# Context passed in a second, turned order and loaded straight to the convolution's operand, in place of transposes on TensorE

## The reference

```
vr, x1r, x2r = v, ctx, ctx reshaped to (B=16, H=32, heads=8, L=512)
kv = vr[:, :, :, None, :] * x2r[:, :, None, :, :]      # 8 x 8 products per (b, h)
y  = causal convolution of kv with k[h] along L        # by FFT in the reference
y  = y + kv * skip[h, i]
out = einsum('bhijl,bhil->bhjl', y, x1r)               # context again
```

## Time and profile before

| what | value |
|---|---|
| median of 3 runs | 1280.31 us (1278.77 to 1292.66) |
| the profiled execution | 1288.01 us, span 1286.1 us |
| mean granted TensorE clock in it | 0.966 |
| TensorE busy | 1158.3 us, 90% of the span |
| VectorE, GpSimd, ScalarE busy | 837.4, 696.6, 547.5 us |
| HBM read, written | 152.65 MB, 43.83 MB |

### The profile page before, as it was taken

One profiled execution on the slowest core, in us unless ns is written; L12 is line 12 of the kernel. 1 busy time (PEld: TensorE's weight loads), 2 busy tenths in 40 slices (PEclk: granted clock), 3 DMA queues, 4 the chain that ended last, 5 costly groups with the idle time before them and its releaser, 6 DMA issues.

```text
span 1286.1 us, 18058 instructions
## 1 busy us (share of the span) xinstructions
PE 1158.3 (90%) x5369; PEld 887.2 (69%) x5369; DVE 837.4 (65%) x1369; ACT 547.5 (43%) x1012; POOL 696.6 (54%) x404
## 2 busy tenths in 40 slices
PE   3999999999999999999689999999888987998893
PEld 2777777777777777777578899996555654665561
DVE  1687787777777777787569994544554544555452
ACT  5455555556555655553411222223433433443341
POOL 4988898889889887995030000012443534445342
PEclk9999999999999999999989999999988989998997
DMA  6313322332233223321366343455999999999994
GB/s 194 86 52 102 102 77 76 102 102 78 75 102 101 80 74 102 102 62 50 107 158 193 98 117 104 122 152 160 277 277 291 290 272 283 289 302 284 283 277 55
DMA packets 88795, 196.51 MB, mean 153 GB/s; under 512 B 14983, under 2 KB 23943, under 8 KB 88624
## 3 DMA queue, kind: packets, MB, share of 16 engines
q1 hardware_dynamic: 73648, 159.84, 43.3%
q0 software_dynamic: 15104, 36.16, 12.3%
HBM read 152.65 MB, written 43.83 MB: 153 GB/s over the span
## 4 chain that ended last, share of the span: by engine, by line
PE 55%; DMA 24%; issue 8%; DVE 7%; ACT 2%; POOL 2%; SPq 1%; POOLq 0%; DVEq 0%; ACTq 0%
DMA out_dram<-o,idx_b 9%; PE Y L541 9%; PE Y L410 8%; DMA out_dram<-w,idx_b 8%; PE Y L412 8%; PE Y L411 8%; PE Y L414 3%; DMA stage<-xn_rows,idx_i 3%; DMA xn<-xn_rows 2%; DVE s L1146 2%; PE DX L393 2%; PE OT L559 2%; PE Y L630 2%; PE DX L559 2%; PE DX L433 2%
## 5 line engine op out<-in xcount | busy, mean ns | idle before, releaser
L969 POOL TENSOR_TENSOR ring<-vT,cT 128x1024 f32<-128x1024 f32 x128 | 249.1, 1957 | 77.9 <-ACT vT L738 49.5
L410 PE MATMUL Y<-split,toep 128*128 128x512 f32 x576 | 250.2, 434 | 9.7 <-POOL split L977 9.7
L1101 DVE TENSOR_TENSOR z<-Y,cT 128x1024 f32<-128x1024 f32 x128 | 156.1, 1220 | 126.8 <-PE Y L414 91.4
L977 POOL TENSOR_TENSOR split<-ring,split 128x1024 fp32r<-128x1024 f32 x96 | 229.8, 2394 | 0.4 <-ACT split L748 0.4
L412 PE MATMUL Y<-split,toep 128*128 128x512 f32 x576 | 228.7, 397 | 0.0
L411 PE MATMUL Y<-split,toep 128*128 128x512 f32 x576 | 228.4, 396 | 0.0
L630 PE MATMUL Y<-ring,xT 128*128 128x384 f32 x512 | 201.5, 520 | 9.1 <-DMA ring<-in_L_ffn_down_proj_dram 7.9
L1013 POOL DMA_INDIRECT stage<-xn_rows,idx_i x64 | 69.1, 1079 | 235.1 <-issue 219.1
L1106 DVE TENSOR_REDUCE o<-z 128x128 f32<-128x1024 f32 x128 | 154.4, 1207 | 1.1
L541 PE MATMUL Y<-split 128*128 128x384 f32 x768 | 152.9, 348 | 1.6 <-DVE split L1160 1.6
L410 PEld LDWEIGHTS Y<-split,toep 128*128 128x128 f32 x576 | 109.2, 190 | 39.4 <-issue 19.1
(11 more groups left out here) (152 smaller groups left out, 1913.1 us busy)
## 6 DMA issues: line engine op xcount, KB each, us to landing
ring<-_L_ffn_gate_up_proj_dram SPq DMA_DIRECT2D x64, 768.0 KB, 7.6
ring<-in_L_ffn_down_proj_dram SPq DMA_DIRECT2D x64, 384.0 KB, 10.2
gr<-filters SPq DMA_DIRECT2D x32, 512.0 KB, 3.8
stage<-in_x_dram SPq DMA_DIRECT2D x32, 256.0 KB, 3.5
stage<-in_ctx_dram SPq DMA_DIRECT2D x32, 256.0 KB, 3.8
x_rows<-stage SPq DMA_DIRECT2D x32, 256.0 KB, 2.9
xn_rows<-xn SPq DMA_DIRECT2D x32, 256.0 KB, 3.0
xn<-xn_rows SPq DMA_DIRECT2D x32, 256.0 KB, 3.8
```

The costliest lines, as they stand in the source:

```text
L410: pe.matmul(y, high, kv[:, s, 0, a, n], start=(a == 0), stop=False)
L969: pool.tensor_tensor(to.rearrange("p (b j i) -> p b j i", i=NH, j=NH), a, d, ALU.mult).then_inc(kvp_ready, 1)
L977: pool.tensor_tensor(kv[:, s, 1, c, :], kvp[c], kv[:, s, 0, c, :].bitcast(F32), ALU.subtract).then_inc(kv_ready, 1)
L1101: dve.tensor_tensor(zz[c % 2].rearrange("p (b j i) -> p b j i", j=NH, i=NH), YY[c % 2][:, :].rearrange("p (b j i) -> p b j i", j=NH, i=NH) ...
```

## The change

The host passes one more input, `turned(ctx)`: for each tile h a block of 128 x 512, whose row p holds, for chunk c and row n of the tile, the context at position c*128 + p. `load_turned(h, s)` copies that block to `cT[:, s]` by one transfer of the sync queue. The eight instructions a tile that made `cT` before are gone from TensorE (four loads of weights and four matmuls, L388), and ScalarE's eviction (L742). GpSimd waits for the transfer in place of the eviction. The wait for `z_done` moves from ScalarE to the sync queue. The loads of tiles 0 and 1 are issued in the set-up, ahead of the wait for `filters_out`; that of tile h+1 stands first in `iteration(h)`, before `load_filter(h + 1)`. The unturned context is loaded as before.

```diff
--- before.py
+++ after.py
@@ -54,7 +54,7 @@
 
 
 def build(nc, x, skip, ctx_in, k, gate_w, gate_up, down, sh_gate, sh_up, sh_down,
-          c_sq, c_order, c_slot, out):
+          c_sq, c_order, c_slot, ctx_turned, out):
     xn_rows = nc.dram_tensor("xn_rows", [T + CAP, LP], F32, kind="Internal").ap()
     x1_rows = nc.dram_tensor("x1_rows", [T, L], F32, kind="Internal").ap()
     chosen_rows = nc.dram_tensor("chosen_rows", [E, CAP], F32, kind="Internal").ap()
@@ -151,6 +151,7 @@
         dve_setup, k_turned, k_high, k_low, filters_out, pads_out = sem("dve_setup"), sem("k_turned"), sem("k_high"), sem("k_low"), sem("filters_out"), sem("pads_out")
         dve_turn, pool_turn = sem("dve_turn"), sem("pool_turn")
         w_ps, w_sb = sem("w_ps"), sem("w_sb")
+        cT_in = [sem("cT_in0"), sem("cT_in1")]
         tile_in, filter_in, g_ready = [sem("tile_in0"), sem("tile_in1")], sem("filter_in"), sem("g_ready")
         skip_in = [sem("skip_in0"), sem("skip_in1")]
         ln1_mean, ln1_var, ln1_sd, ln1_rstd = sem("ln1_mean"), sem("ln1_var"), sem("ln1_sd"), sem("ln1_rstd")
@@ -158,7 +159,7 @@
         skip_ready = sem("skip_ready")
         b_xT_lo, b_hT_lo, sh_lo = sem("b_xT_lo"), sem("b_hT_lo"), sem("sh_lo")
         v_ready, w_ready = sem("v_ready"), sem("w_ready")
-        vT_ps, cT_ps, dx_ps, vT_sb, cT_sb = sem("vT_ps"), sem("cT_ps"), sem("dx_ps"), sem("vT_sb"), sem("cT_sb")
+        vT_ps, dx_ps, vT_sb = sem("vT_ps"), sem("dx_ps"), sem("vT_sb")
         kv_ready, conv_done, z_done, o_done = sem("kv_ready"), sem("conv_done"), sem("z_done"), sem("o_done")
         dc_ready, xr_ready, oT_ps, x1_ready = sem("dc_ready"), sem("xr_ready"), sem("oT_ps"), sem("x1_ready")
         ln2_stats, ln2_mv, ln2_sd, ln2_rstd = sem("ln2_stats"), sem("ln2_mv"), sem("ln2_sd"), sem("ln2_rstd")
@@ -230,6 +231,11 @@
                 sp.dma_start(xt[:, s, :], rows(x_f, h)).then_inc(tile_in[s], 16)
                 sp.dma_start(ct[:, s, :], rows(c_f, h)).then_inc(tile_in[s], 16)
 
+            def load_turned(h, s):
+                if not among(h, 0, 1):
+                    sp.wait_ge(z_done, (h - 1) * NC)
+                sp.dma_start(cT[:, s, :, :].rearrange("p c n -> p (c n)"), ctx_turned[h]).then_inc(cT_in[s], 16)
+
             def load_filter(h):
 
                 parts, whole = filters[h, 0, 0:L], filters[h, 2, L - P:L]
@@ -251,7 +257,9 @@
             for part in range(2):
                 sp.dma_start(filters[:, part, :], kparts[part].bitcast(F32)).then_inc(filters_out, 16)
             sp.dma_start(filters[:, 2, :], kpad).then_inc(filters_out, 16)
+            load_turned(0, 0)
             load_rows(1, 1)
+            load_turned(1, 1)
             sp.dma_start(slot_c[:], c_slot).then_inc(small_in, 16)
             sp.wait_ge(filters_out, 48)
             load_filter(0)
@@ -277,6 +285,8 @@
                 load_skip(h, s)
 
             def iteration(h, s):
+                if not among(h, 0, NT - 1):
+                    load_turned(h + 1, 1 - s)
                 if not among(h, NT - 1):
                     sp.wait_ge(g_ready, h + 1)
                     load_filter(h + 1)
@@ -384,10 +394,6 @@
                 for c in range(NC):
                     last = pe.transpose(TA[:, c * P:(c + 1) * P], v[:, s, c * P:(c + 1) * P], ident)
                 last.then_inc(vT_ps, 1)
-                for c in range(NC):
-                    last = pe.transpose(TB[:, c * P:(c + 1) * P], ct[:, s, c * P:(c + 1) * P], ident)
-                last.then_inc(cT_ps, 1)
-
                 pe.wait_ge(w_ready, h + 1)
                 pe.wait_ge(skip_ready, h + 1)
                 pe.matmul(DX[:, :], skip_b[:, s, :], w[:, s, :], start=True, stop=True).then_inc(dx_ps, 1)
@@ -434,16 +440,14 @@
                 last.then_inc(logit_ps, 1)
 
             def turn_weights(n):
-                if n == 0:
-                    pe.wait_ge(cT_sb, NT)
-                elif n == 1:
+                if n == 1:
                     pe.wait_ge(sc_ready, NT - 2)
                     pe.wait_ge(xr_ready, NT)
                 elif n in (4, 5):
                     pe.wait_ge(z_done, NC * NT - 1)
                 elif n in (7, 8):
                     pe.wait_ge(z_done, NC * NT)
-                else:
+                elif n:
                     before = max(m for m in range(n) if turn_bank[m] is turn_bank[n])
                     pe.wait_ge(sh_lo, before + 1)
                 if n < 2 * NC:
@@ -465,7 +469,6 @@
                 conv(h, s, 0, 1)
                 if not among(h, NT - 1):
                     pe.wait_ge(vT_sb, h + 1)
-                    pe.wait_ge(cT_sb, h + 1)
                     if not among(h, 0, 1):
                         pe.wait_ge(xT_sb, h - 1)
                         pe.wait_ge(sc_ready, h - 1)
@@ -736,10 +739,6 @@
                 if not among(h, 0, 1):
                     act.wait_ge(kvp_ready, (h - 1) * NC)
                 act.activation(vT[:, s, :, :].rearrange("p c n -> p (c n)"), TA[:, :], ACT.Copy).then_inc(vT_sb, 1)
-                act.wait_ge(cT_ps, h + 1)
-                if not among(h, 0, 1):
-                    act.wait_ge(z_done, (h - 1) * NC)
-                act.activation(cT[:, s, :, :].rearrange("p c n -> p (c n)"), TB[:, :], ACT.Copy).then_inc(cT_sb, 1)
 
             def kv_high_part(h, s, c):
                 act.wait_ge(kvp_ready, h * NC + c + 1)
@@ -957,7 +956,7 @@
             def product(h, s, c):
                 if c == 0:
                     pool.wait_ge(vT_sb, h + 1)
-                    pool.wait_ge(cT_sb, h + 1)
+                    pool.wait_ge(cT_in[s], landed(h, s, 16))
                 if c < NC - 1:
                     if not among(h, 0):
                         pool.wait_ge(kv_ready, (h - 1) * (NC - 1) + c + 1)
@@ -1468,6 +1467,11 @@
     return {"sq": sq, "order": order.reshape(P, T // 2), "slot": np.arange(P, dtype=np.float32).reshape(P, 1)}
 
 
+def turned(ctx):
+
+    return ctx.reshape(B, NT, NH, NC, P).transpose(1, 4, 3, 0, 2).reshape(NT, P, L)
+
+
 def kernel(**inputs):
     import numpy as _np
     import concourse.bacc as _bacc
@@ -1477,6 +1481,7 @@
     nc = _bacc.Bacc("TRN2", target_bir_lowering=False, num_devices=1)
     arrays, args = {}, []
     data = [(name, inputs[name]) for name in _INS] + list(constants().items())
+    data.append(("turned", turned(_np.asarray(inputs["ctx_2048"]))))
     for name, value in data:
         a = _np.ascontiguousarray(value)
         arrays[f"in_{name}_dram"] = a
```

## The result

The changed kernel takes **1315.39 us** (median of 4 runs, 1309.45 to 1321.29) against 1279.54 us of the kernel before (4 runs); the ratio is 1.0257 with a 95% interval of 1.0172 to 1.0343. A second measurement of the same two kernels, with 6 and 11 runs, gave 1.0169 (1.0125 to 1.0212). So it is slower by some 2%, as forecast; the 4.1% of the forecast (1333 us) was too much.

What follows compares the result with a forecast made beforehand. TensorE, plus some late xn, was taken as the bound; after, a ring: 30 x 20.2 - 553.8 = +52 us, plus 1.5 at the start, on the profiled 1288.0 gives 1341.7, about 1333 us against the median; range 1300 to 1362.

Steps and rivals of the forecast that it cites:

- Removed: Four context transposes leave TensorE, 0.44 us a tile, 14.1 us in all; ScalarE's context eviction goes, its next instruction 0.48 us earlier.
- the gain rival: TensorE stays the bound: 14.1 us of transposes and up to 12.3 us of stalls go, 1254 to 1266 us; chance 0.05.
- Moved: Sync queue: filters wait behind the turned load until after z, VectorE's last product of a tile; formerly issued at z - 3.7 us.
- The ring: From z through filters, ScalarE, GpSimd, roots, xn and transposes to the next z: 20.2 us a tile, against 18.46 before.
- step 2: Issue of the turned load, then filters, until ScalarE turns them (L725): 5.57 us, read from 5.13 and 6.39.
- step 1: From z, the end of VectorE's last product of a tile, to the turned load's issue: 0.17 us.
- Steps 3 to 6: L725 to GpSimd's first product 2.03 us; second copy and roots 3.90, 0.96, 0.25; xn 0.92; transposes 1.48; next z 4.92.
- The sign of being wrong: Forecast wrong if filters land within 4.2 us of the turned load's issue, or L427's wait is not the last to end.
- The price from the Trainium skill: Step 2 by 2.0 us plus bytes over 436 GB/s: 3.95 us for 852 kB, ring 18.6 us, time about 1285 us.
- The short leg: Rival: step 2 is 4.5 us, ring 19.2, time 1303 us; within 1% needs under 4.2 us; chance 0.09 for that.
- The clock: Rival: gaps of 2.6 us lower TensorE's clock, up to 1.5 us a tile more, 1345 to 1380 us; chance 0.06 above range.
- The copy L1146: VectorE's copy of six scores, 0.16 or 1.16 us before, would take 0.16 us throughout, at about z + 6.3 us.

Runs made afterwards that it cites:

- filters first: Changed kernel with the next tile's filters issued ahead of the turned load and its wait on the sync queue: 1258.64 us, ratio 0.9795; again 1254.09 us, 0.9699.
- wait without bytes: Changed kernel, order and wait kept, but from tile 2 on the turned load brings 16 of 512 columns: 1304.31 us, ratio 1.0153.
- bytes without wait: Kernel before, plus the turned load ahead of the filters into an unread spare buffer, without the wait for z: 1284.73 us, ratio 0.9984.

## Why the prediction was right

The mechanism held in each step, the size did not: the time lies 18 us below the forecast, inside its range of 1300 to 1362 us. (The sum as worked out comes to 1334 us against the median, not 1333.)

- **Removed.** Right where nothing else is in the way (17.4 us a tile with filters first, where the kernel before had 17.8 to 17.9 in its short tiles), and right that in the changed kernel the saving falls into idle time. What the removal is worth alone was less than the gain rival said, since the copy's stalls stay and grow more frequent. With filters first they are short (at most 1.03 us from 100 to 600 us) because GpSimd is still at its pair when the copy is due; that the rival's 12.3 us for them came in there too is luck of timing.
- **Moved.** Right: the filters behind *z* are the cause. The swap shows it from one side, the two halves (wait without bytes, bytes without wait) from the other.
- **The ring.** 20.2 us was forecast, 19.36 measured. The term that was mis-sized is step 2, from the issue of the turned load to L725. I took 5.57 us from the `xn` store with filters behind it; together with step 1 that is 5.74 us after *z*, and the mean behind tiles 2 to 28 was 4.9, that is, 4.7 us for step 2 (4.3 to 5.6). The turned load occupies the queue for 0.35 us and the filters follow 0.53 us after its start, where the store's 0.60 and 0.84 were taken; and the filters land 3.4 us from their issue (the second transfer 3.5), the median, against 3.7 and 4.0 for the second. That they land sooner for want of an `x1` store just ahead is not shown; with filters first, where the stores are back ahead of them, it is 3.7 again. Steps 3 to 6 sum to 14.3 us in the tile shown against 14.5 forecast. The whole difference is 0.8 us a tile, 25 of the 32 us between the forecast for the profiled execution (1341.7 us) and its 1309.45. TensorE's wait for `xn` was accordingly 1.5 us a tile and 38.3 us in all, where 2.6 and 75 were said.
- **The rest of that gap** is the 5.8 us after the stage and a start that cost nothing: *z* of tile 0 came at 48.00 us in both profiles, where 1.5 us had been added.
- **The sign of being wrong** (filters landed within 4.2 us of the turned load's issue) came close. The first filter transfer alone does land within it, 0.53 + 3.4 = 3.9 us; the second, which ScalarE also needs, at 4.6 us does not.
- **The price from the Trainium skill.** As an estimate, the fit of the Trainium skill, "DMA: Bandwidth & Descriptors", section "Anatomy of one DMA — SWDGE (gpsimd) path", which is for another path, gave 3.95 us for step 2. The trace has 4.69 in the tile shown. The measurement lies about midway between the fit and my reading of the store; the sum by the fit (1285 us, no change) is 30 us below the result, mine 18 above it.
- **The short leg** (rival, no change): the leg was shorter than I had it, but no change needed one under 4.2 us; the leg that came, 4.7, is near the one it named, and its 1303 us are nearer to the result than my 1333.
- **The clock** (rival): it occurred in part, inside my range, not above it. The stage table of the kernel after behind one of its two longest waits, and that wait:

```profile
393.00:397.00 4.00, 4.00 (x14) 3.34 (x14) 0.84 (x1) 2.29 (x5) 4.00 (x3) 0.62 0.25 66
397.00:414.00 17.00, 15.31 (x72) 11.27 (x71) 12.83 (x23) 7.58 (x14) 12.20 (x7) 1.00 0.33 96
```

```profile
392.76 1.08 PE L433 MATMUL TA<-sq,xn 128*128 128x128 f32 x4 [2.29 <-ACT xn L757]
```

  Behind a wait of 2.29 us the granted clock is 0.62 of full speed over 4 us, that is, for some three quarters of them at 1.2 GHz, and the next *z* follows after 6.43 instead of 4.92 us. Two tiles of 30 had it: some 3 us in all, where the rival had up to 1.5 us in every tile.
- **The copy L1146** takes 0.16 us in the median tile after, 0.80 before, as forecast; one of 26 from 100 to 600 us still took 1.91 us. The waits that it caused are gone, and the ring has put its own, 38.3 us, in their place.

## What to carry to other kernels

A load that must wait for a buffer to come free belongs behind what is needed sooner on its queue, or on another queue; its own bytes cost nothing while the filters went out in time, and the filters behind its wait cost 4.6% against the same kernel with the two loads swapped (1312.03 and 1254.09 us on one chip). Follow a moved wait round until it meets itself: a delay that closes a ring within one tile is paid in every tile, and the sum of the ring's terms is the period. When one link of a ring is shortened, look for the wait that was just met before: it comes next, and it may act on another engine than the one that shows it.

## What the runs showed of the hardware

- VectorE's copy of 128 x 6 elements takes 0.16 us when GpSimd is idle and up to 2.42 us when it isn't, and then ends with GpSimd's instruction. Due while one of GpSimd's products ran, it ended with that product (up to 1.9 us); due just after the pair, with the subtraction behind it (2.1 to 2.4 us). With transposes, eviction and the per-tile load gone, the long case came in 13 of 28 tiles instead of 9 of 27. With filters first, where GpSimd waits for a transfer (21.8 us in 17 waits), it came in none; that this wait is the reason is read from the trace, not tested.
- The granted clock of TensorE fell behind waits of 2.07 to 2.31 us (five in two profiles, 0.57 to 0.68 over the 4 us that follow), and that cost some 1.5 us each on top of the wait; behind another wait of 2.21 us it stayed at 1.00.
- The issue of a 256 KB load with rows of 2 KB in one block took 0.33 to 0.35 us of the sync queue in most tiles; that of 256 KB of rows in the strided order 0.54 to 0.69 us.
